# Cross-attention, self-attention and experts on one core: expert regions zeroed in fixed pieces during attention, and the written-out order planned anew

## What is computed

```python
x = x + tanh(g_xattn) * cross_attention(layernorm(x), ctx, ctx)      # 16 heads of 16
z = layernorm(x)
s = ln(z + self_attention(z), ln1)                                    # 16 heads of 16
gates = softmax(s @ gW + gb); w = top 2 of 8 experts, by their gates
y = sum over the 2 experts e of  w_e * (relu(s @ W1[e] + b1[e]) @ W2[e] + b2[e])
out = x + tanh(g_ffn) * ln(s + y, ln2)
```

## Time and profile before

| | |
|---|---|
| median of 3 runs | 1215.42 us |
| the profiled execution | 1216.49 us |
| its span | 1214.7 us |
| TensorE busy | 1126.1 us, 93% |
| VectorE, ScalarE busy | 827.8 us, 688.4 us |
| GpSimd busy | 265.8 us, 22% |
| DMA queue of SyncE | 54.24 MB, 16.2% of 16 engines |

### The profile page before, as it was taken

The page is one execution under the profiler, slowest core; times in us unless marked ns, Lnnn a source line. Parts: engine busy times, 40 slices in busy tenths (PEclk is TensorE's granted clock), DMA queues, the critical chain, the costliest instruction groups (busy, mean ns, idle before and its releaser), DMA issues.

```text
span 1214.7 us, 36448 instructions
## 1 busy us (share of the span) xinstructions
PE 1126.1 (93%) x12924; PEld 840.5 (69%) x12925; DVE 827.8 (68%) x2431; ACT 688.4 (57%) x1186; POOL 265.8 (22%) x371
## 2 busy tenths in 40 slices
PE   6999999999999999999999999999728999999964
PEld 4576766676766666676666677667517999999942
DVE  5565777776777777667777776777744666666667
ACT  4666767677666667777667776776513333333200
POOL 1011111122212111222212221222321222222233
PEclk9999999999999999999999999999968999999988
DMA  6012043222111111111111011101056222222165
GB/s 149 22 42 68 17 123 105 69 68 74 40 33 37 51 34 33 38 41 34 33 53 38 10 45 46 30 28 64 28 116 187 71 69 71 72 72 71 52 212 159
DMA packets 66597, 79.18 MB, mean 65 GB/s; under 512 B 14008, under 2 KB 52536, under 8 KB 66328
## 3 DMA queue, kind: packets, MB, share of 16 engines
q1 hardware_dynamic: 52680, 54.24, 16.2%
q0 software_dynamic: 6096, 15.66, 3.9%
q10 hardware_dynamic: 7680, 7.34, 1.9%
HBM read 51.32 MB, written 25.90 MB: 64 GB/s over the span
## 4 chain that ended last, share of the span: by engine, by line
PE 75%; issue 9%; DVE 8%; ACT 4%; POOL 1%; DMA 1%; DVEq 0%; another core or an unknown queue 0%; SPq 0%; POOLq 0%; ACTq 0%
PE quad L1299 11%; PE bank L1289 10%; PE bank L1485 9%; PE quad L1497 9%; PE quad L1311 8%; PE sums L1322 6%; PE bank L1436 4%; PE bank L1389 4%; ACT probs L777 4%; PE quad L1308 3%; PE bank L1282 3%; PE bank L1457 2%; PE bank L1322 2%; DVE row_max_C L1050 2%; DVE row_max_C L1047 2%
## 5 line engine op out<-in xcount | busy, mean ns | idle before, releaser
L777 ACT ACTIVATE probs<-quad 125x1792 f32<-125x1792 f32 (+1 forms) x128 | 213.0, 1664 | 116.9 <-PE quad L1311 116.7
L855 ACT ACTIVATE scored_half<-quad 112x750 bf16<-112x750 f32 (+1 forms) x160 | 131.4, 821 | 89.5 <-PE quad L1299 89.0
L1037 DVE TENSOR_REDUCE row_max_A<-quad 112x2 f32<-112x750 f32 x128 | 120.1, 938 | 70.0 <-PE quad L1299 66.5
L1485 PE MATMUL bank<-tile_inT,tile_w 128*128 128x128 f32 x1008 | 124.4, 277 | 0.3 <-ACT tile_w L887 0.3
L1039 DVE TENSOR_REDUCE row_max_A<-scored_half 112x2 f32<-112x750 bf16 x128 | 118.6, 927 | 3.2 <-ACT scored_half L855 1.0
L1485 PEld LDWEIGHTS bank<-tile_inT,tile_w 128*128 128x128 f32 x1008 | 119.0, 194 | 0.7 <-ACT tile_w L887 0.7
L1497 PE MATMUL quad<-output_w,hiddenT 128*128 x504 | 119.1, 380 | 0.0
L1299 PE MATMUL quad<-kT_A,qT_A 32*112 32x375 f32 x1024 | 115.2, 519 | 3.5 <-ACT probs L777 1.5
L1216 DVE TENSOR_SCALAR hiddenT<-bank,hidden_b 128x128 f32<-128x128 f32 x252 | 71.0, 344 | 63.0 <-PE bank L1485 62.6
L1289 PE MATMUL bank<-ctxT,wxk 128*128 128x375 f32 x256 | 99.1, 510 | 5.5 <-DMA bxk<-in_bxk_dram 5.5
L739 POOL DMA_INDIRECT kept_dram<-tile_out,take_back x63 | 60.4, 959 | 186.3 <-DVE tile_out L1239 179.7
(11 more groups left out here) (225 smaller groups left out, 1995.0 us busy)
## 6 DMA issues: line engine op xcount, KB each, us to landing
ctxT<-in_ctxT_dram SPq DMA_DIRECT2D x32, 375.0 KB, 3.5
tile_in<-sent_dram SPq DMA_DIRECT2D x63, 129.0 KB
join_in<-kept_dram SPq DMA_DIRECT2D x28, 256.0 KB, 3.4
hidden_w<-in_hidden_w_dram SPq DMA_DIRECT2D x8, 512.0 KB, 5.0
output_w<-in_output_w_dram SPq DMA_DIRECT2D x8, 512.0 KB, 5.7
x_in<-in_x_dram SPq DMA_DIRECT2D x32, 112.0 KB, 2.9
x_res<-in_x_dram SPq DMA_DIRECT2D x32, 112.0 KB, 3.2
kept_dram<-x_shift SPq DMA_DIRECT2D x32, 112.0 KB
```

The costliest lines, as they stand in the source:

```text
L777: act.activation(probs[0:rows, t.buffer("probs", step), :, :], quad[0:rows, :, 0:U * T], ACT.Exp, scale=SCALE).then_inc(taken[kind_of(step ...
L855: act.activation(scored_half[:, t.buffer("half", step), 0:RT // 2 * n].rearrange("t (r s) -> t r s", s=n), quad[0:T, RT // 2:RT, 0:n], ACT ...
L1037: dve.tensor_reduce(row_max["A"][:, i:P // 2:ROWS], quad[0:T, 0:RT // 2, 0:S], AX_X, ALU.max).then_inc(taken[kind], 1)
L1485: mm = pe.matmul(hidden_bank[k][:, f * P:(f + 1) * P], tile_w[:, k, c, f * P:(f + 1) * P], tile_inT[:, k, c, :], start=c == 0, stop=c == D ...
```

## The change

The looked-up zeroing goes, with its cast, its semaphores and its wait. In its place all regions are zeroed, in 33 pieces: piece j is rows j*112 to (j+1)*112 of all eight regions (piece 32 the last 128 rows), as two DMAs of half a row each. From item 4 on, each N.load on SyncE is followed by one or two pieces, behind the loads of x, context and, in the early turns, weights; SyncE waits once for `zero_row`. E.send of item n waits for pieces 0 to n (the last item for all 33). The three buffers of cross-attention values are all cleared in S.set, and in FIRST the first N.ln and S.mask stand ahead of S.set. SyncE loads the key bias ahead of the key weights. ORDER, FIRST and LAST are new throughout; N.load and F.load in ORDER are now at +0 and +1 instead of +3, and E.send at -1 instead of -2. In the diff, most of FIRST and LAST is left out.

```diff
@@ -46,8 +46,7 @@
 REGION = NB * T + P
 
 
-LAST_KNOWN = NB - 3
-BEHIND = (NB - 1 - LAST_KNOWN) * T + P
+FIRST_CLEAR = 4
 NT = NB * T * TOP // P + E - 1
 
 
@@ -176,48 +175,48 @@
 PROBS = 4
 
 ORDER = [
-    "A.k0", "M.mT-1", "B.s2-1", "D.pv-1", "E.gate-1", "B.pv1-1", "N.ln-1", "E.pick-1", "E.rank-1", "B.pv2-1",
-    "E.copy-2", "B.s0", "A.k1", "F.oN", "A.xT", "X.max", "A.q", "E.send-2", "E.oN", "A.v0", "F.norm-1", "E.aT",
-    "M.max0", "F.aT", "F.res", "E.out", "B.s1", "F.out", "A.v1", "M.max1", "F.shift-1", "C.yT", "B.pv0", "N.load+3",
-    "M.max2", "F.load+3", "C.qk0", "X.mT", "M.max3", "C.qk1", "C.bias-1", "C.v", "E.norm", "D.s"]
+    "F.shift-1", "N.ln-1", "B.pv2-1", "B.s0", "F.oN", "A.xT", "F.norm-1", "A.k1", "X.max", "A.q", "E.oN", "A.v0",
+    "X.mT", "E.send-1", "E.aT", "M.max0", "C.bias-1", "F.aT", "E.out", "B.s1", "F.out", "A.v1", "M.max1", "C.yT",
+    "N.load", "B.pv0", "M.max2", "C.qk0", "C.v", "M.max3", "E.norm", "C.qk1", "F.res+1", "D.s", "A.k0+1", "E.gate",
+    "F.load+1", "M.mT", "E.pick", "B.s2", "E.rank", "E.copy", "D.pv", "B.pv1"]
 
 FIRST = """
-    A.k0 A.xT S.set A.k1 A.q A.v0 N.ln S.mask N.ln M.max0 A.k0 M.max1 M.max2 A.v1 A.xT M.max3 A.k1 A.q N.load M.mT
-    B.s0 A.v0 M.max0 B.s1 N.load A.v1 B.pv0 N.ln M.max1 N.ln B.pv1 N.load A.xT B.s2 N.load A.k0 M.max2 B.pv2 M.max3
...
+    A.k0 A.xT N.load N.ln S.mask S.set A.k1 A.q A.k0 N.ln M.max0 M.max1 A.xT A.k1 N.load M.max2 A.q M.max3 A.v0
+    M.max0 M.mT A.v1 M.max1 A.v0 B.s0 A.v1 B.s1 W.fold N.ln B.s2 A.k0 N.load A.k1 M.max2 B.pv0 B.pv1 A.xT M.max3 A.q
...
 LAST = """
...
-    F.norm C.qk1 C.v D.pv E.oN X.max C.yT E.aT E.gate F.shift E.send C.qk0 C.bias X.mT E.out E.norm E.send D.s C.qk1
-    E.pick E.rank D.pv E.gate E.oN E.pick E.copy E.copy E.rank X.max E.aT X.mT E.out E.send D.s E.norm C.v D.pv
-    E.gate E.oN E.pick E.aT E.rank F.shift E.copy E.out E.copy E.norm E.send E.gate E.pick E.rank E.send""".split()
...
+    X.max C.yT E.oN C.v E.aT X.mT E.gate E.out D.s E.pick C.qk0 E.norm E.rank F.shift C.qk1 E.gate X.max D.pv E.oN
+    X.mT E.send C.v E.pick E.copy E.aT E.rank D.s E.out D.pv E.norm E.oN E.copy E.gate E.aT E.pick E.send E.rank
+    E.out E.copy E.norm E.gate E.pick E.send E.rank E.copy E.send""".split()
@@ -557,15 +554,6 @@
                         keys_over(sp)
                         sp.dma_start(output_b[:, :], io["output_b"].rearrange("e d -> (e d)").partition_broadcast(P)
                                      ).then_inc(output_b_loaded, DMA)
-                    elif step == "E.rank" and t.item("E") == LAST_KNOWN:
-
-                        sp.wait_ge(rows_zeroed, 5)
-                        sp.wait_ge(rows_known, 1)
-                        for e in range(E):
-                            row_no = sp.value_load(next_i[0:1, e:e + 1], min_val=e * REGION, max_val=e * REGION + (LAST_KNOWN + 1) * T)
-                            sp.dma_start(io["sent"][bass.ds(row_no, BEHIND), :].rearrange("(p r) (h d) -> p (r h) d", r=4, h=2),
-                                         zero_row[0:BEHIND // 4, :].unsqueeze(1).to_broadcast([BEHIND // 4, 8, SENT // 2])
-                                         ).then_inc(tails_zeroed, DMA)
                     elif step == "F.shift":
                         n, k = t.item("F"), t.slot("F")
                         sp.wait_ge(shifted, t.item("F", 1, 1))
@@ -573,8 +561,8 @@
 
             def load_weights(stage):
                 if stage == "K":
+                    column(bxk, io["bxk"]).then_inc(w_loaded["K"], DMA)
                     square(wxk, io["wxk"]).then_inc(w_loaded["K"], DMA)
-                    column(bxk, io["bxk"]).then_inc(w_loaded["K"], DMA)
                 if stage == "Q":
                     square(wxq, io["wxq"]).then_inc(w_loaded["Q"], DMA)
                     column(bxq, io["bxq"]).then_inc(w_loaded["Q"], DMA)
@@ -597,11 +585,25 @@
                         row(b, io[a]).then_inc(w_loaded["C"], DMA)
                     sp.dma_start(gate_w[:, :, :], io["gate_w"].rearrange("(c p) e -> p c e", p=P)).then_inc(w_loaded["C"], DMA)
 
+            def clear(j):
+
+                rows = T if j < NB else REGION - NB * T
+                regions = io["sent"][:, :].rearrange("(e r) d -> r e d", e=E)
+                for half in (slice(0, SENT // 2), slice(SENT // 2, SENT)):
+                    sp.dma_start(regions[j * T:j * T + rows, :, half],
+                                 zero_row[0:rows, :].unsqueeze(1).to_broadcast([rows, E, SENT // 2])).then_inc(regions_zeroed, DMA)
+
             def turn(t):
                 move(t)
                 n = t.item("N")
                 if t.only != "N.load":
                     return
+                if n == FIRST_CLEAR:
+                    sp.wait_ge(rows_zeroed, 5)
+                if n >= FIRST_CLEAR:
+                    cleared = [(NB + 1) * m // (NB - FIRST_CLEAR) for m in (n - FIRST_CLEAR, n - FIRST_CLEAR + 1)]
+                    for j in range(*cleared):
+                        clear(j)
                 for stage in ("KQV", "BC")[n] if n < 2 else ():
                     load_weights(stage)
                 if n == 6:
@@ -719,8 +721,7 @@
                         pool.wait_ge(xm_copied, t.item("E", 1, 1))
                         pool.wait_ge(row_steps, t.item("E", 6, 6))
                         settled(pool, passed_pool)
-                        if t.item("E") > LAST_KNOWN:
-                            pool.wait_ge(tails_zeroed, E * DMA)
+                        pool.wait_ge(regions_zeroed, (t.item("E") + 1 if t.item("E") < NB - 1 else NB + 1) * 2 * DMA)
                         for i in range(TOP):
                             pool.indirect_dma_start(out=io["sent"], out_offset=bass.IndirectOffsetOnAxis(
                                 ap=send_row[:, k, i:i + 1], axis=0), in_=xm[:, k, i, :], in_offset=None).then_inc(sent[k], DMA)
@@ -907,7 +908,8 @@
         def _(dve):
             def prepare():
 
-                dve.memset(values["A"][:, DEEP["A"] - 1, :, :, :], 0.0).then_inc(vset, 1)
+                for i in range(DEEP["A"]):
+                    dve.memset(values["A"][:, i, :, :, :], 0.0).then_inc(vset, 1)
                 for k in range(DEEP["C"]):
                     dve.memset(values["C"][:, k, :, :, :], 0.0).then_inc(vset, 1)
                 dve.wait_ge(vset, DEEP["A"] + DEEP["C"])
@@ -1106,8 +1108,6 @@
                         dve.tensor_reduce(route[:, 0:TOP], rows_pick[:, :, :], AX_X, ALU.add).then_inc(row_steps, 1)
                         dve.wait_ge(row_steps, t.item("E", 6, 5))
                         dve.tensor_copy(send_row[:, k, :], route[:, 0:TOP]).then_inc(row_steps, 1)
-                        if t.item("E") == LAST_KNOWN:
-                            dve.tensor_copy(next_i[:, :], next_row[:, :]).then_inc(rows_known, 1)
                     elif step == "F.out":
                         dve.wait_ge(made["F.out"], t.count(step))
                         dve.wait_ge(res_shifted, t.item("F", 1, 1))
@@ -1160,8 +1160,6 @@
                         dve.scalar_tensor_tensor(xm[:, k, 0, 0:D], r_gain[:, :], inv_std["E"][:, :], ln1_b[0:T, :],
                                                  ALU.mult, ALU.add).then_inc(gained, 1)
 
-            for i in range(DEEP["A"] - 1):
-                dve.memset(values["A"][:, i, :, :, :], 0.0).then_inc(vset, 1)
             ATTENTION.run(dve, turn)
             keys_over(dve)
```

More of the change, by code:

```diff
@@ L189 @@
-    N.load B.s1 F.oN A.v0 M.max0 A.v1 F.aT C.yT M.max1 A.k0 B.s2 C.qk0 F.out M.max2 C.qk1 C.bias W.gate2 M.max3
-    F.norm N.load F.shift A.q A.k1 M.mT X.max A.xT B.pv0 B.s0 C.bias X.mT C.v F.shift A.q M.max0 C.yT B.pv1 B.pv2
-    M.max1 C.qk0 F.oN N.ln D.s A.k0 C.v M.max2 D.pv F.aT B.s1 F.res F.out B.pv0 M.max3 B.pv1 E.oN B.s2 M.mT A.k1
-    C.qk1 F.res M.max0 B.pv2 F.norm E.aT B.s0 A.k0 A.xT F.oN X.max C.yT F.aT B.pv0 B.s1 C.qk0 E.out B.s2 F.out C.v
-    X.mT M.max1 F.res B.pv1 B.pv2 F.norm E.norm D.s F.oN C.yT C.qk1 M.max2 D.pv N.load M.max3 C.qk0 E.oN F.load M.mT
@@ new lines @@
+    A.k1 F.shift F.load N.ln M.mT X.max B.pv1 C.v B.s0 F.out A.xT F.res B.pv2 F.norm B.s1 A.k0 F.oN C.yT M.max0 A.q
+    C.v M.max1 A.v1 F.aT F.res M.max2 C.qk0 X.mT M.max3 C.qk1 N.load F.out D.s B.pv0 B.pv1 D.pv F.shift B.s2 F.shift
+    M.mT E.oN F.norm A.k1 X.max B.pv2 N.ln C.yT E.aT B.s0 F.oN F.res A.v0 M.max0 F.aT E.out X.mT B.s1 F.load E.norm
+    C.qk0 B.pv0 D.s F.out A.k0 E.gate M.max1 A.k1 C.bias C.qk1 M.max2 D.pv M.max3 F.norm A.xT A.v1 B.s2 B.pv1 M.mT
+    A.q E.pick E.oN X.max N.load F.shift B.pv2 B.s0 X.mT C.v F.oN E.aT M.max0 E.out C.bias F.aT B.s1 A.v0 E.copy
```

52 lines of the change are left out of this document (25 added, 27 removed).

## The result

The kernel after takes 1230.90 us, median of 4 runs (1228.07 to 1233.26), against 1215.58 before: ratio 1.0129 [1.0117, 1.0141], where 1200 was forecast. The profiled execution took 1228.07 us, span 1226.3.

| us | before | after | difference |
|---|---|---|---|
| up to x_norm(7) | 165.66 | 168.25 | +2.6 |
| 17 steady turns, to x_norm(24) | 454.7 | 473.8 | +19.1 |
| drain, to the last cast | 277.0 | 275.3 | -1.6 |
| seam, to the first tile on TensorE | 18.19 | 8.17 | -10.0 |
| experts and join | 299.2 | 300.8 | +1.6 |

What follows compares the result with a forecast made beforehand. Attention was taken as bound by TensorE's work, with idle time at the drain's end and seam. -10.65 + 0.7 - 1.5 - 3.0 - 1.5 = -15.95 from 1216.49 gave 1200.5, stated as 1200; range 1194 to 1210, own range 1196 to 1204.

Steps and rivals of the forecast that it cites:

- The zeroing: SyncE's load turns: 66 fixed transfers of 3.53 us each fit in the turn of 26.77 us; cost taken as 0.7 us.
- what waits behind them: SyncE's queue: residual load, x1 store and next item's loads fit beside the zeroing, 22.3 of 26.77 us, so 0.
- The row that I leaned on: Steady turns from 233.01 to 259.78 us: 1 MB more of expert weights loaded, turns with and without it alike.
- The upper bound of 233 us: Cost of the added zeroing if none of its 66 transfers of 3.53 us were hidden.
- the hidden end: Lower bound of the zeroing's cost, 0 where all is hidden; 0.7 us was taken, near it.
- Rival (b): SyncE's queue: zeroing starves attention's loads, up to 1282.5 us, decisive over 5.4 us a transfer; mild drain form 1203 to 1208; chance 0.10.
- The seam: Between attention and experts: without the wait for looked-up zeroing the first tile load comes at 902.7, saving 10.65 us.
- The steady turns: Attention's repeated turns: reordering fills TensorE's wait for att_E; -3.0 us, bounds -3.9 and +3.
- The start: Kernel start: first norm ahead of the memsets ends TensorE's wait of 1.96 us; -1.5 us, bounds +0.5 to -2.5.
- its bound of +0.5 us: Kernel start: worst case for the early norm, with A.v0 left undone while S.set holds the maxima.
- The drain: Fill and drain orders: X.max(31) before E.rank(29), D.s(31) before E.out(30); -1.5 us, bounds -4 to +3.
- Start, fill and drain together: Two terms of -1.5 us each: the early first norm, and the new fill and drain orders.

Runs made afterwards that it cites:

- the ten pieces: The kernel after with 10 of its 33 zeroing pieces, one in a turn, 23 left out: 1199.32 us, ratio 0.9878; run again on another chip 1193.32 us, ratio 0.9912.
- the new order with the look-up: The kernel after, its orders and start kept, with the eight looked-up zeroing transfers of the kernel before in place of the fixed pieces: 1213.16 us, ratio 0.9993.
- the reads: The kernel after with 10 zeroing pieces in single issues, plus bursts of eight 512 KB weight reads at N.load 14, 16, 18 and 20: ratio 0.9921.

## Why the prediction was wrong

- *The zeroing: failed.* "They fit, so 0 ... I take 0.7 us" measured 30 us for 46 of the 66 transfers (1226.3 - 1196.6 = 29.7 in span; 18 on the last chip, where both were timed side by side). Not its durations: a transfer takes 2.4 us, not 3.53, and the turn's queue does fit. Two rules of the Trainium skill, "DMA: Bandwidth & Descriptors", were weighed there. That a transfer of 112 partitions is split over 16 engines ("Why a DMA increments its semaphore by 16 and not by 1") gave an estimate of 2.4 us, and the trace agrees. That a row pitch of 4 MiB halves the rate ("Latency and other measured facts") gave an estimate of 7.1 us. That row of the page is of pitches that are powers of two, and this one is 3.83 MB; no halving shows at it. The step that failed is "what waits behind them": I listed SyncE's own transfers and no other user of the DMA engines, and TensorE's instruction packets are one: seven of them came too late in the steady turns, for 12.1 us of idleness and up to 10.7 more at and behind them, most of it at the half clock. The row that I leaned on, turns with and without 1 MB of weights being alike, was of a burst of reads about 6 us long; with zeroing beside it the burst was 12 to 21. The upper bound of 233 us was no guide, and the hidden end rested on one row.
- *Rival (b)* had the right part and sign but not the mechanism or the size: loads did not starve (TensorE never waits for ctxT in the turns; a store did hold up the drain, with the old order), the price is not set at 5.4 us a transfer, and 0.07 for slower was too little for a change with 66 transfers whose neighbours on the engines had not been listed.
- *The seam: right.* -10.65 forecast, -10.0 measured; the chain is the one forecast.
- *The steady turns: right in kind, small in size.* -3.0 forecast, -6.7 in 17 turns (454.7 to 448.0), of which the wait for att_E is one part.
- *The start: its steps right, its gain not there.* TensorE's wait of 1.96 us is gone and VectorE's first maxima start at 17.87 (17.9 forecast). But x_norm(7) comes at 166.74 in the ten pieces and at 167.04 in the new order with the look-up, 1.1 to 1.4 us later than before, where start and fill together were to be 1.5 earlier. The wait came back in another place: VectorE, busy with the memsets, is now late with the first maxima, and TensorE, which is there earlier, waits for them. Before, the kernel after, and the new order with the look-up:

```profile
21.63 0.90 PE L1299 MATMUL quad<-kT_A,qT_A 32*112 32x375 f32 x8 [1.06 <-DVE row_max_A L1037]
```
```profile
18.85 1.61 PE L1297 MATMUL quad<-kT_A,qT_A 32*112 32x375 f32 x8 [3.75 <-DVE row_max_A L1039]
```
```profile
18.31 1.27 PE L1298 MATMUL quad<-kT_A,qT_A 32*112 32x375 f32 x8 [2.75 <-DVE row_max_A L1038]
```

Around this wait the granted clock is 0.50 in both (17.9 to 24.7 in the kernel after, 18.7 to 22.1 with the look-up), which before's start has not. The forecast saw such a wait as its bound of +0.5 us, "A.v0 left undone while S.set holds the maxima", and took the gain. How much of the 1.1 to 1.4 us this wait is, no run says.

- *The drain: right in sign, small in size.* -1.5 forecast (with the fill past the start), -4.0 in the ten pieces (273.0 against 277.0).
- *Start, fill and drain together* come to -2.9 against -3.0. That is luck: +1.1 and -4.0 for -1.5 and -1.5.
- *Experts:* 0 forecast, +1.5 in the ten pieces (300.7 against 299.2), with 0.2 to 2.0 in the other kernels; not looked into.

Without the zeroing's stops the sum looks as if it had stood, -15.95 forecast and -15.15 measured for the ten pieces (1214.47 to 1199.32), but that is in part luck. The misses of the parts cancel, the parts as read from the two profiled executions add up to -18.1 in span (1214.7 to 1196.6), and on the last chip the ten pieces give only -10.3 (1203.65 to 1193.32).

## What to carry to other kernels

Before calling a DMA hidden, list all who use the DMA engines in that stretch, instruction packets of q8 and q14 among them, and not only the queue that it stands in. Put added transfers one at a time where the queue is idle: the same 46 transfers cost 18 to 30 us in bursts and about 0.5 in single pieces half a turn apart. In a trace, an engine that stops in mid-step, on the same instruction in each run, with "issue" as the releaser, is a sign of late instructions. Count its records up to the stop and the packets of the instruction queue: here the stops lie at every 256th record, counted from 193. Look there for a burst, and add to its price what TensorE loses while busy (here 10.7 us beside 15.3 of idleness), most of it at the half clock.

## What had not been expected

- Stops of 1.1 to 4.1 us in TensorE, each at the first instruction of a packet, behind bursts of 10 us and more.
- Writes in 516-byte packets run at 192 GB/s, and the expert weights at about 370 (1.85 MB from 372 to 377 us in the reads); 4.2 MB of the latter at a time cost 0.4 us in four turns.
- Chips differ in this: the bursts' price was 30 us between the first two traces and 18 us on the last chip, with undisturbed turns of 26.4 on both, though the kernel before is 11 us faster on the last (1203.65 against 1214.47).
